# A hand-written order for attention with an image prompt: the fifth group of each batch rearranged

## What is computed

```python
q, k_t, v_t = heads(x @ W_q), heads(text @ W_k), heads(text @ W_v)
probs_t = softmax(q @ k_t.T * scale)
text_out = probs_t @ v_t
scores_ip = q @ heads(ip @ W_k_ip).T * scale
qsem = l2norm(probs_t @ text)                 # per head, 512 wide
probs_ip = softmax(scores_ip + 0.5 * qsem @ l2norm(ip).T) * mask
out = text_out + probs_ip @ heads(ip @ W_v_ip)
out = out @ W_out + b_out + x
```

## Time and profile before

| | us |
|---|---|
| median of 3 runs | 407.01 |
| lowest and highest run | 405.26, 410.0 |
| the profiled execution, its time | 406.1 |
| the profiled execution, its span | 404.3 |

### The profile page before, as it was taken

One profiled execution on the slowest core, in us unless ns is written; L12 is line 12 of the kernel. 1 busy time (PEld: TensorE's weight loads), 2 busy tenths in 40 slices (PEclk: granted clock), 3 DMA queues, 4 the chain that ended last, 5 costly groups with the idle time before them and its releaser, 6 DMA issues.

```text
span 404.3 us, 9496 instructions
## 1 busy us (share of the span) xinstructions
PE 387.9 (96%) x3631; PEld 318.2 (79%) x3631; DVE 226.4 (56%) x509; ACT 204.8 (51%) x486; POOL 207.8 (51%) x220
## 2 busy tenths in 40 slices
PE   8999998999999999999999999999999999999985
PEld 5548888778788878887889878887888878877763
DVE  0798363665466535665465646664566646654443
ACT  1433234564646573546356554557455466467722
POOL 3020280282637772586437562787257443845972
PEclk9999999999999999999999999999999999999998
DMA  8499986357205702372218420480208210000000
GB/s 262 137 266 240 243 153 124 104 160 120 70 2 174 125 13 73 105 154 42 84 21 202 75 59 26 151 146 14 73 2 172 50 41 2 2 13 29 3 14 18
DMA packets 29456, 38.04 MB, mean 94 GB/s; under 512 B 14361, under 2 KB 26745, under 8 KB 28729
## 3 DMA queue, kind: packets, MB, share of 16 engines
q1 hardware_dynamic: 28514, 36.36, 37.5%
q10 hardware_dynamic: 896, 1.07, 0.9%
HBM read 28.50 MB, written 8.81 MB: 92 GB/s over the span
## 4 chain that ended last, share of the span: by engine, by line
PE 84%; ACT 3%; POOL 3%; DMA 3%; issue 3%; DVE 3%; SPq 1%; ACTq 0%; POOLq 0%; DVEq 0%
PE PR L955 41%; PE Y L955 26%; PE P L955 8%; PE O L955 6%; DMA et<-ctxT 2%; ACT big L703 1%; PE PR L1113 1%; POOL el L570 1%; DVE cTl L924 1%; POOL t L587 1%; DMA qst<-ma 1%; POOL pb L565 1%; ACT cTh L751 1%; PE PR L1050 0%; DVE el L770 0%
## 5 line engine op out<-in xcount | busy, mean ns | idle before, releaser
L565 POOL TENSOR_TENSOR pb<-pb 128x448 f32<-128x448 f32 x78 | 89.1, 1142 | 100.3 <-DVE pb L852 94.8
L830 DVE TENSOR_REDUCE mx<-PR 112x1 f32<-112x371 f32 x160 | 83.8, 539 | 80.2 <-PE PR L955 79.0
L955 PE MATMUL Y<-er,Gh 128*128 128x448 f32 x240 | 96.9, 404 | 1.2 <-DVE pb L852 0.6
L852 DVE TENSOR_TENSOR pb<-big,Y 128x448 f32<-128x448 f32 x120 | 72.9, 620 | 36.9 <-PE Y L955 35.6
L955 PE MATMUL Y<-er,Gl 128*128 128x448 f32 x240 | 87.3, 364 | 0.0
L703 ACT ACTIVATE big<-P 128x448 f32<-128x448 f32 x120 | 65.2, 543 | 28.2 <-PE P L955 27.6
L707 ACT ACTIVATE er<-big 128x448 fp32r<-128x448 f32 x120 | 69.4, 578 | 3.8
L955 PEld LDWEIGHTS Y<-er,Gh 128*128 128x128 f32 x240 | 45.2, 188 | 11.8 <-DVE pb L852 7.5
L955 PE MATMUL PR<-kst,qst 96*112 96x371 bf16 x160 | 51.0, 330 | 0.9 <-DVEq L806 0.8
L955 PEld LDWEIGHTS Y<-er,Gl 128*128 128x128 f32 x240 | 45.2, 189 | 2.6
L955 PE MATMUL P<-qst,kst 99*128 99x112 bf16 x480 | 43.6, 213 | 1.0 <-DMA qst<-ma 0.9
(11 more groups left out here) (170 smaller groups left out, 661.2 us busy)
## 6 DMA issues: line engine op xcount, KB each, us to landing
et<-ctxT SPq DMA_DIRECT2D x8, 752.0 KB, 4.4
kst<-kd SPq DMA_DIRECT2D x7, 720.0 KB, 7.7
kd<-ks SPq DMA_DIRECT2D x16, 288.0 KB, 2.9
qst<-qd SPq DMA_DIRECT2D x48, 70.0 KB, 2.5
kst<-kd SPq DMA_DIRECT2D x7, 480.0 KB, 9.7
kst<-kd SPq DMA_DIRECT2D x9, 240.0 KB, 9.1
qd<-kst SPq DMA_DIRECT2D x4, 336.0 KB, 6.0
vx<-xr SPq DMA_DIRECT2D x8, 140.0 KB, 2.3
```

Source lines behind the costliest of these rows:

```text
L565: pool.tensor_tensor(total, total, (pz, pm)[j], ALU.add).then_inc(s_S, 1)
L830: dve.tensor_reduce(mx[b % 2][:, h:h + 1], bank[0:S, 0:T], AX.X, ALU.max).then_inc(s_free[seq[u] % NR], 1)
L852: dve.tensor_tensor((pz, pm, pa[g % 2])[j], eb[g % 3][:, 448 * j:448 * j + 448], Y[y % 2][:, 0:448], ALU.mult).then_inc(s_P, 1)
L955: return pe.matmul(o, st, mv, start=start, stop=stop, **kw)
```

## The change

Only the order of the units changes; every unit does the same as before. In the fifth group of batches 1 to 4 (ROUNDS) the three Gram tiles are no longer parted by pT and ip: g2 and g1 run together, pT stands before g0, v moves ahead of S0 and ip comes directly behind it. S1 moves ahead of cT. The output projection o leaves the group; as the new word "o-" it stands in the first group of the next batch, behind its S0 and K0. In LATE (batches 5 and 6) the order is the same but o stays at the end of the group. In the last batch pT moves ahead of v, ip ahead of g2, cT from behind g1 to behind g2 and with that ahead of r0' and pw', and o ahead of g0.

```diff
@@ -48,23 +48,23 @@
 
 
 
-ROUNDS = ("S0 K0 m g m K1 S1 m v S2 m G0 m",
+ROUNDS = ("S0 K0 o- m g m K1 S1 m v S2 m G0 m",
           "S0 m g m K2 m S1 v m S2 G1 m",
           "S0 m g2 T0 T1 g1 g0 m r0 G2 m S1 m pw v S2 m V0",
           "Kr S0 r1 m g m V1 m S1 m m v r2 mT S2 z V2",
-          "p E g2 pT g1 ip g0 S0 cT S1 v S2 o")
+          "p E g2 g1 pT g0 v ip S0 S1 cT S2")
 SECOND = "K0 S0 m g m K1 S1 m v S2 m G0 m"
 EARLY = ("m m S0 m g m K1 S1 m S2 K2 m",
          "S0 m g m S1 m S2 v m m wo",
          "S0 m g m S1 m v S2 V0 m",
          "Kr S0 m g m V1 m S1 m m v S2 mT V2",
          "E g S0 v S1 S2")
-LATE = "p g2 pT g1 ip g0 S0 cT S1 v S2 o"
+LATE = "p g2 g1 pT g0 v ip S0 S1 cT S2 o"
 LAST = ("S0 g2 S1 g1 g0 S2 v T0 T1",
         "S0 r0 pw g2 S1 g1 g0 S2 v",
         "S0 r1 g2 S1 g1 r2 g0 S2 v",
-        "S0 z g2 p S1 g1 g0 S2 v pT T0'",
-        "g2 ip r0' pw' g1 cT g0 o r1' v vW r2' z' p'")
+        "S0 z g2 p S1 g1 g0 S2 pT v T0'",
+        "ip g2 cT r0' pw' g1 o g0 r1' v vW r2' z' p'")
 
 
 def master_schedule():
@@ -106,6 +106,8 @@
                 unit.update({"T0": ("T", f, 0), "T1": ("T", f, 1), "pw": ("pw", f, 0), "r0": ("r", f, 0, 0), "r1": ("r", f, 0, 1),
                              "r2": ("r", f, 0, 2), "z": ("z", f, 0), "p": ("p", f, 0), "pT": ("pT", f), "ip": ("ip", f), "cT": ("cT", f),
                              "o": ("o", f)})
+            if 2 <= b < B - 2:
+                unit["o-"] = ("o", f - 1)
             if n == B:
                 unit.update({"vW": ("vW", b)})
                 unit.update({"T0'": ("T", b, 0), "pw'": ("pw", b, 0), "r0'": ("r", b, 0, 0), "r1'": ("r", b, 0, 1),
```

## The result

The changed kernel takes 416.27 us (median of 4 runs, 415.45 to 418.08), the kernel before 406.13 beside it: ratio 1.0237, 95% interval 1.0159 to 1.0316. It is slower, as forecast, but by 10 us and not by 6.4. The forecast was 413.4; the measured median lies 0.3 above the upper end of the range, 416.0.

The account below looks back on a forecast made before the run. TensorE's order of work was taken to set the end (matmuls fill 96% of the span). Ordinary borders 2.3, LATE 4.1 and last batch 0 gave +6.4, on 407.0 us 413.4; range 407.5 to 416.

Parts of the forecast that it names:

- Ordinary border: Behind batches 1 to 4: S0 waits for ScalarE (+0.17), VectorE delays g0 (+0.4); four times, +2.3 us.
- LATE border: Behind batches 5 and 6: o 7.84 after g2's start (G), not 5.77, 2.4 us idle; +2.07 each, +4.1 together.
- Last batch: Kernel's end: POOL's residual add leaves the chain (-0.87), r0' reciprocal 0.8 later behind cT's low parts; near 0.
- rival (c): Granted clock drops in LATE's 2.4 us idle, work then at 1.2 GHz: 415.8 or 418.2 us; chance 0.06.
- Rival (a): S0 of next group: ScalarE not in the way, S1's exp by G+4.8 (G: g2's start); 406.4 us; chance 0.10.
- Rival (b): LATE stalls partly given back under the last batch's waits, ordinary borders nearly even: 409.8 us; chance 0.10.
- Rival (d): The move hides and costs nothing, o's and K0's lengths only change places: 407.0 us; chance 0.05.

Follow-up runs that it names:

- the first experiment: The changed kernel with the LATE string put back as before, ordinary borders and last batch still changed: 409.18 us, ratio 1.0045 to the kernel before.
- the swap: The changed kernel with cT ahead of S1 in LATE, v left where the change puts it: 411.94 us, ratio 1.0119 to the kernel before.

## Why the prediction was right, and where it fell short

**Ordinary border.** Forecast: m 10.22 behind g2, S0 of the next group late and released by ScalarE's exp. After (g2, S0, m and g0 of one border):

```profile
185.76 0.37 PE L957 MATMUL Y<-er,Gh 128*128 128x448 f32 x1
...
192.01 0.37 PE L957 MATMUL P<-qst,kst 99*128 99x112 bf16 x4 [0.47 <-ACT big L705]
...
195.92 0.36 PE L957 MATMUL PR<-kst,qst 96*112 96x371 bf16 x1
...
198.90 0.47 PE L957 MATMUL Y<-er,Gh 128*128 128x448 f32 x1 [0.61 <-DVE pb L854]
```

10.16 from g2 to m, and the wait with the releaser that was named (it shows 0.47; the rest of the gap is the tail of S2's record). g0 was put 0.4 later than before; at another border m and g0, then VectorE's o sum, K0 residual, maximum and product of g2:

```profile
241.03 0.36 PE L957 MATMUL PR<-kst,qst 96*112 96x371 bf16 x1
...
243.65 0.48 PE L957 MATMUL Y<-er,Gh 128*128 128x448 f32 x1 [0.25 <-DVE pb L854]
```

```profile
241.13 0.49 DVE L946 TENSOR_TENSOR res<-PR,res 112x320 f32<-112x320 f32 x1 [2.47 <-PE PR L957]
241.84 0.55 DVE L805 TENSOR_TENSOR kr<-PR,ks 128x372 f32<-128x372 f32 x1 [0.21 <-DVE res L946]
242.53 0.55 DVE L832 TENSOR_REDUCE mx<-PR 112x1 f32<-112x371 f32 x1
242.99 1.14 DVE L854 TENSOR_TENSOR pb<-big,Y 128x448 f32<-128x448 f32 x2
```

2.62 against 2.25: +0.37, and the order and gaps on VectorE are those that were added up from the earlier trace rows, with 0.21 behind the sum and 0.14 behind the residual, while the product starts 0.09 before the maximum's record ends. At the border shown first the gap behind the sum was 0.57 and g0 came 2.98 behind m, in the first experiment's trace too; I can't explain that. The Trainium skill, VectorE: DVE Perf Modes ("The DRAIN you can't avoid"), says that semaphores between chained VectorE operations cost nothing extra; this trace does not agree where VectorE waits for its own last operation. Sum of the four: forecast +2.3, measured +2.0 in the traces and +1.8 by the first experiment. It is divided otherwise than forecast, though: m is only 0.3 later over the four borders (forecast 0.7, but at the fourth the order before had taken 10.21, not 10.05), and g0 another 1.9 (forecast 1.6). So VectorE's order is nearly all of this cost, and that the sum came so close is in part luck.

**LATE border.** Forecast o at G+7.84, 2.4 us idle; measured 7.93, 2.15 idle (2.33 from the end of S2's 0.18, as the forecast counts) and 0.34 before cT. That ScalarE's written order holds o back is shown by the swap, which moved o by 1.04 as expected; that is half of the stall.

**Last batch.** Forecast near 0, by two moves of 0.8 and 0.87 that cancel. POOL's part after (L628 is the residual add, L589 the power):

```profile
396.08 0.87 POOL L628 TENSOR_TENSOR res<-vx,bias 112x320 f32<-112x320 f32 x1
...
398.91 2.28 POOL L589 TENSOR_TENSOR t<-ssq,halfm 112x12 f32<-112x12 f32 x1
```

The residual add is out of the chain, ahead of r0' and the power, and the power starts 0.8 later than before, counted from the last S2 (398.91 - 392.16 = 6.75, before 388.73 - 382.78 = 5.95). Alone these strings are even.

**The step that failed** is the weight of rival (c), the clock. It was named, placed in the idle time of LATE, and priced at 415.8 to 418.2, that is 8.8 to 11.2 over its base of 407.0, and the measured 10.1 over 406.13 lies there; but it got a chance of 0.06 and stands at nothing in the likeliest sum. The reason given, that no idle as long as this stood in the rows, was a reason for not knowing, and I read it as a reason for leaving the sum at full clock. The two dips cost 4.4 us, a term as large as the two stalls (4.3) behind which they came. With it the sum is 6.4 + 4.4 = 10.8; the traces have 9.5, or 10.6 without the quicker start. The Trainium skill, TensorE: Matmul & The Clock Gate (Part 1, "What's actually happening"), says that the clock has two states, 1.2 and 2.4 GHz, and that idle time takes it down; the rows agree on the two levels (0.50 and 1.00), and the experiment with the idle time filled on what takes it down.

Rival (a) is wrong at its place: the exp of S1 starts 326.01 - 320.34 = 5.67 behind g2, where it needed 4.8. Rival (b) too: nothing was given back in the last batch but 0.3 us behind the second dip, 0.1 of which the end lost again. Rival (d) falls by the measured time and the wait of S0 that is new.

## What to carry to other kernels

Here TensorE was busy nearly all of the time, and the change of order could be priced by what lies between an instruction and the return of its result on the other engines, counted in those engines' own written order; moving v and ip "directly" to their new places took the cover from cT and o. A border with a ready unit (K0) in that gap was faster than either order of the dependent units without it. A stall of TensorE can have a second price, the clock: 2.15 us of idle had it at all four borders profiled, 0.91 us had not in the one trace. It belongs into the sum as a term with two cases and not only among the rivals.

## What was not expected of the hardware

The granted clock fell behind each of the four borders with 2.15 us of idle time that were profiled (two in the changed kernel, two with the LATE string alone), and late: three times while o was running, once some 0.3 us before it started. It stayed at 0.50 for about 3.4 us once and about 6.8 us in the other three, though TensorE was busy throughout, so the loss after one stall was 1.4 to 3.1 us, more than half of the stall or more than all of it. With the same stretch filled by useless matmuls it did not fall behind either border of the profiled run. Why the length of the dip differs between borders stays open.
